# First period of the last layers, batch beside batch, and the loads and gathers ahead of it

## What is computed

```
x = LN(x + attn0(x));  x = LN(x + xattn0(x, ctx));  x = LN(x + experts(x))       # layer 0, top 2 of 8 experts
x = LN(x + attn1(x));  x = LN(x + xattn1(x, ctx));  x = LN(x + mixer(x))         # layer 1: "the last layers"

attn1: xn = layernorm(x) * g + b
  q, k = l2norm(xn Wq), l2norm(xn Wk), both rotated (rope);  v = xn Wv
  gcp  = exp(clip(cumsum(-softplus(xn Wgate + bg)), -60, 50))
  pe   = exp(p - max over tokens of p) * softplus(xn Wclock + bc),   p = xn Wp + bp
  q = q * gcp / (cumsum(pe) + 1e-8);   k = k * pe / (gcp + 1e-8)
  out = causal softmax(q k / 4) v per head (16 heads of 16);  x1 = out Wo + bo + x
  result = x1 + MLP(layernorm(x1))
```

## Time and profile before

| what | us |
|---|---|
| median of 3 runs | 1316.02 (1314.69 to 1317.96) |
| profiled execution, its own time | 1315.13 |
| its span, first to last instruction | 1313.1 |
| PE busy | 1121.8 (85%) |
| DVE busy | 738.3 (56%) |
| ACT busy | 537.9 (41%) |
| POOL busy | 454.8 (35%) |

### The profile page before, as it was taken

How to read it: one execution, slowest core, us unless ns; L and a number is a source line. 1 busy time by engine, 2 the same in 40 slices (tenths; PEclk the granted TensorE clock), 3 DMA queues, 4 the chain that set the end, 5 groups by cost and what they waited for, 6 DMA issues and landing times. The chain is left out here.

```text
span 1313.1 us, 20231 instructions
## 1 busy us (share of the span) xinstructions
PE 1121.8 (85%) x6714; PEld 786.2 (60%) x6714; DVE 738.3 (56%) x2210; ACT 537.9 (41%) x1385; POOL 454.8 (35%) x548
## 2 busy tenths in 40 slices
PE   7889988997898886899999734776997899899996
PEld 3456456545644665899999712543664575467775
DVE  1472476248435825465555427657549676846366
ACT  1371255217323711333333125464465556534541
POOL 0150034005201576666666343224132522222022
PEclk9999999999999997899999957698998999899999
DMA  5000200020001040811111170001000100000000
GB/s 190 17 1 1 55 17 1 0 55 17 1 0 55 1 158 17 301 49 50 50 49 49 34 229 8 25 1 30 3 9 1 32 2 24 1 1 25 0 1 32
DMA packets 40226, 52.37 MB, mean 40 GB/s; under 512 B 10780, under 2 KB 33372, under 8 KB 40124
## 3 DMA queue, kind: packets, MB, share of 16 engines
q1 hardware_dynamic: 31100, 36.66, 8.8%
q0 software_dynamic: 3408, 9.31, 2.5%
q10 hardware_dynamic: 5616, 5.11, 1.2%
HBM read 41.76 MB, written 9.31 MB: 39 GB/s over the span
## 5 line engine op out<-in xcount | busy, mean ns | idle before, releaser
L1281 PE MATMUL bank<-words 128*128 128x256 f32 (+3 forms) x848 | 275.4, 476 | 31.7 <-ACT words L1792 17.3
L1281 PEld LDWEIGHTS bank<-words 128*128 128x128 f32 (+1 forms) x848 | 159.7, 195 | 122.0 <-issue 66.9
L358 PE MATMUL bank<-words 128*128 128x512 f32 x384 | 173.1, 602 | 8.3 <-DMA words<-in_wq 8.3
L324 POOL TENSOR_TENSOR words<-words 128x256 f32<-128x256 f32 (+1 forms) x128 | 103.6, 831 | 190.5 <-DVE words L700 190.5
L876 PEld LDWEIGHTS bank<-words 128*128 128x128 f32 x1248 | 147.7, 194 | 4.2 <-ACT words L910 2.3
L876 PE MATMUL bank<-words 128*128 128x128 f32 x1248 | 148.2, 278 | 1.6 <-ACT words L910 1.6
L571 ACT ACTIVATE words<-words 128x128 f32<-128x128 f32 (+1 forms) x256 | 113.3, 444 | 50.2 <-DVE words L695 50.2
L358 PEld LDWEIGHTS bank<-words 128*128 128x128 f32 x384 | 72.5, 193 | 90.6 <-issue 90.0
L553 ACT ACTIVATE words<-bank 128x512 f32<-128x512 f32 x48 | 28.7, 598 | 192.5 <-PE bank L358 192.5
L925 ACT ACTIVATE words<-words 128x1024 f32 x39 | 41.2, 1057 | 146.4 <-PE bank L876 113.1
L610 DVE COPY words<-bank 128x512 f32<-128x512 f32 x48 | 33.2, 691 | 106.2 <-PE bank L358 105.9
(11 more groups left out here) (263 smaller groups left out, 2035.5 us busy)
## 6 DMA issues: line engine op xcount, KB each, us to landing
words<-in_w SPq DMA_DIRECT2D x8, 1024.0 KB
y_slots<-words ACTq DMA_DIRECT2D x39, 128.0 KB
words<-in_w SPq DMA_DIRECT2D x8, 512.0 KB
words<-in_xt SPq DMA_DIRECT2D x4, 512.0 KB, 3.8
words<-in_x SPq DMA_DIRECT2D x4, 512.0 KB, 4.2
x_rows<-words SPq DMA_DIRECT2D x16, 128.0 KB
words<-in_wm SPq DMA_DIRECT2D x2, 1024.0 KB, 6.5
out_x<-words SPq DMA_DIRECT2D x16, 128.0 KB, 1.8
```

What stands on the lines that cost most here:

```text
L324: last = pool.tensor_tensor(part, part, inv[:, j % SLOTS0, :, t:t + 1].to_broadcast([P, 2, P * (t + 1)]), ALU.mult)
L358: last = pe.matmul(bank[c % 2][:, :], w, r, start=k == 0, stop=k == KD - 1)
L1281: last = pe.matmul(out, w, r, start=i == 0, stop=i == len(pairs) - 1)
```

## The change

1. **Loads moved.** The ten loads of `rows` and `early` stand at the end of SP's queue in the experts' block, into a region at the top of SBUF that is kept free (`Memory.limit`). POOL's copy of the slots and the memsets of `minus_half` and `eps` stand at the end of its queue in that block.
2. **Boundary.** The experts' block is opened with `no_gpsimd_drain=True`.
3. **Gathers by tile.** The gathers' order is tile by tile, both choices of a tile together. In period 0 DVE takes statistics and normalises by halves (`front_half`, `front_rows_of`); for group 1 too, in two halves.
4. **Roots.** The second norm's variance is worked out on DVE (v/(v+eps)+eps, four small steps of which each has a drain ahead of it); POOL makes both roots in one `pow` (`front_rstd`). This holds for every group.
5. **Constants.** POOL writes them after the two roots of period 0; `va` waits for the four normalised tiles. ACT and DVE still wait for `const` ahead of the forms' reads and the gate; PE no longer ahead of the first turn.
6. **Period 0 by batches.** Forms, gates, factors and attention of period 0 are written out for batch 0 and batch 1, on all engines, each step on 256 columns; DVE's factors of batch 1 stand between the minima of batch 0. Rotated tiles, squares and q/k banks get places of their own (`firstra`, `firstrb`, `firstsq`, `FIRSTQK`), since batch 0's attention runs while batch 1's are alive.
7. Periods 1 to 3 keep their order; their counts are shifted (`forms_of`, `gates_of`, `squares_of`).

```diff
-        block = ctx.enter_context(nc.Block())
+        block = ctx.enter_context(nc.Block(no_gpsimd_drain=True))
...
+            for name in ("bm1", "cols", "rope", "parity"):
+                part = keep["l_" + name]
+                sp.dma_start(part[:, :] if name in ("bm1", "parity") else part[:, :, :], dram[name]).then_inc(keep["rows"], 16)
...
+            for name in ("wgate", "wclock", "wpp", "wqk", "wv1"):
+                sp.dma_start(keep["l_" + name][:, :, :], dram[name].rearrange("(k p) n -> p k n", p=P)).then_inc(keep["early"], 16)
...
-                for n in range(2 * NT):
+                for n in (r * NT + t for t in range(NT) for r in range(2)):
...
+            def front_rstd(g, b=None):
+
+                h = tiles_of(b)
+                pool.wait_ge(n3.stats, front_count(g, b))
+                pool.tensor_tensor(powers[:, 2:4, h], powers[:, 0:2, h], minus_half[:, 2:4, h], ALU.pow).then_inc(n3.rstd, 1)
+
+            front_rstd(0, 0)
+            front_rstd(0, 1)
+            constants()
+            pool.wait_ge(rows, NR * 16)
+            for b in range(GB):
+                pool.wait_ge(uready, b + 1)
+                pool.tensor_tensor(csum[:, :, batch(b)], csum[:, :, batch(b)], clog[:, :, batch(b)], ALU.add).then_inc(clogged, 1)
+                for t in range(NT)[rows_of(b)]:
+                    pool.wait_ge(turning, t + 1)
+                    pool.tensor_tensor(firstrb[:, t, :], firstrb[:, t, :], firstra[:, t, :], ALU.add).then_inc(swung, 1)
+            pool.wait_ge(vmm, NT)
+            gather(1)
...
+            for b in range(GB):
+                pe.wait_ge(turning, HALF * b + HALF)
+                first_turns(b)
+                pe.wait_ge(qkt, HALF * b + HALF)
+                for j in range(PAIRS1 // GB + 3):
+                    if j < PAIRS1 // GB:
+                        scores(0, (PAIRS1 // GB * b + j,))
+                    if j >= 3 and j % 2:
+                        weighted(0, QUADS1 // GB * b + (j - 3) // 2)
+            turn_front(1)
...
+            act.wait_ge(const, 1)
+            first_forms(0)
             front_turned(0, 1)
+            first_rows(0)
+            first_gate(0)
+            first_forms(1)
+            first_factors(0)
+            first_rows(1)
+            first_gate(1)
+            for j in range(PAIRS1):
+                if j >= 4 and j % 2 == 0:
+                    heads_copy(0, (j - 4) // 2)
+                if j == PAIRS1 // GB:
+                    first_factors(1)
+                exponential(0, j)
...
+            for t in range(HALF):
+                combine(0, t)
+                combine(0, NT + t)
+            front_half(0, 0)
+            combine(0, 2)
+            combine(0, NT + 2)
+            front_rows_of(0, 0)
+            combine(0, 3)
+            combine(0, NT + 3)
+            front_half(0, 1)
+            front_rows_of(0, 1)
...
             dve.wait_ge(const, 1)
+            first_gate(0)
+            first_max(0)
+            square_sums(0, 0)
+            first_clock(0)
+            square_sums(0, 1)
+            first_norms(0)
+            first_sums(0)
+            first_gate(1)
+            first_keys(0)
+            first_rotations(0)
+            first_max(1)
+            first_factors(0)
+            minimum(0, 0)
+            minimum(0, 1)
+            square_sums(0, 2)
+            minimum(0, 2)
+            minimum(0, 3)
+            first_clock(1)
+            minimum(0, 4)
+            square_sums(0, 3)
+            minimum(0, 5)
+            first_norms(1)
+            first_sums(1)
+            minimum(0, 6)
+            minimum(0, 7)
+            first_keys(1)
+            first_rotations(1)
+            first_factors(1)
+            for j in range(PAIRS1 // GB, PAIRS1):
+                minimum(0, j)
+                combine(1, j - PAIRS1 // GB)
+            front_statistics(1)
+            front_normalise(1)
```

More of the change, by code:

```diff
@@ new lines, in first_rows, with first_gate @@
+            def first_rows(b):
+                square(0, HALF * b)
+                value_copy(0, HALF * b)
+                value_copy(0, HALF * b + 1)
+                act.wait_ge(pmaxed, b + 1)
+                for c in range(KD):
+                    last = act.activation(pexps[:, c, batch(b)], pexps[:, c, batch(b)], ACT.Exp, bias=pmax[:, GB * c + b:GB * c + b + 1])
+                last.then_inc(pexp, 1)
+                square(0, HALF * b + 1)
+            def first_gate(b):
+                part = batch(b)
+                act.wait_ge(clr, b + 1)
+                act.activation(gabs[:, :, part], gsum[:, :, part], ACT.Exp, scale=-1.0)
+                act.drain()
+                act.activation(gabs[:, :, part], gabs[:, :, part], ACT.Ln, bias=tiny[:, :])
+                act.drain()
+                act.activation(gabs[:, :, part], gabs[:, :, part], ACT.Exp, scale=-1.0).then_inc(ginv, 1)
@@ new lines, in _, with first_gate @@
+            for t in range(HALF):
[9 more added lines that the diff above has]
+            front_rows_of(0, 1)
+            def first_gate(b):
+                dve.wait_ge(lgate, b + 1)
+                for m in range(KD):
+                    dve.tensor_tensor_scan(gsum[:, m, batch(b)], gsum[:, m, batch(b)], gabs[:, m, batch(b)], 0.0, ALU.add, ALU.add)
+                dve.drain()
+                dve.tensor_scalar(gsum[:, :, batch(b)], gsum[:, :, batch(b)], -50.0, 60.0, ALU.max, ALU.min).then_inc(clr, 1)
@@ new lines, in first_clock, with first_sums @@
+            def first_clock(b):
+                dve.drain()
+                dve.wait_ge(clogged, b + 1)
+                dve.tensor_tensor(csum[:, :, batch(b)], csum[:, :, batch(b)], qfac[:, :, batch(b)], ALU.subtract)
+            def first_sums(b):
+                dve.drain()
+                dve.wait_ge(pexp, b + 1)
+                dve.tensor_tensor(pexps[:, :, batch(b)], pexps[:, :, batch(b)], csum[:, :, batch(b)], ALU.mult)
+                dve.drain()
+                for m in range(KD):
+                    last = dve.tensor_tensor_scan(qfac[:, m, batch(b)], ones[:, :], pexps[:, m, batch(b)], 0.0, ALU.mult, ALU.add)
+                last.then_inc(sumr, 1)
@@ L2251, in _ @@
+            for p in range(1, PERIODS):
                 a, r, z = stages(p)
```

378 lines of the change are left out of this document (250 added, 128 removed).

## The result

The changed kernel takes 1304.49 us (median of 4 runs, 1303.3 to 1306.38), the one before 1316.92 in the same comparison (4 runs): ratio 0.9916, 95% interval 0.9902 to 0.9931, 12.4 us less (by the interval 9.1 to 12.9). The forecast was 1301, 15.3 less, in a range of 1294 to 1310. The profiled execution of the changed kernel has a span of 1304.6 and a time of 1306.38, 1.9 over its median.

A forecast was written before the change was run, and what follows sets the result against it. No engine was taken as the bound, but an order in which batches 0 and 1 pass each step together. 1315.13 - 3.3 (boundary) - 12.0 (period 0's stages) = 1299.8, set to 1301 us for the median; range 1294 to 1310.

The forecast's parts named there:

- The boundary: Between last y store and first gather: taking out the drain saves 3.3 us, bounds 0 and -3.7.
- The entry: Last block's first instruction to ACT's first read of a form: 20.5 us instead of 27.7, saving 7.2.
- `const` is late next: End of the entry: POOL's constants come last, and ACT waits 6 us for them.
- Forms to scores: ACT's first read of a form to batch 0's first scores: 31.8 us instead of 47.5, saving 15.7.
- The clamp beside POOL's sum: Forms to scores, on DVE: clamp priced at 1.2 us from the trace; by the page alone, 0.2.
- Scores to period 1: First scores to period 1's first product: 45.9 us instead of 35.0, costing 10.9, with batch 1's factors between batch 0's minima.
- Periods 1 to 3: After period 0: order kept, gains stay; DVE's extra small steps in periods 1 and 2 cost 0, bounds -2 and +2.
- The first two: Period 0's TensorE clock: 1.2 GHz all through, 1314.7 us, chance 0.12; or staying at 2.4 GHz, 1295 us, chance 0.12.
- what the prediction held against cutting them: Products cut in halves: idle gaps between short bursts bring TensorE's clock back down, by the Trainium skill's rule.
- The second: Rival: TensorE stays at 2.4 GHz in period 0; batch 1's quads save 3.2 us, the rest 2.5; 1295 us, chance 0.12.
- The third: Rival at the boundary: the wait isn't removed but moves; 1304 us, chance 0.08.
- The fourth: Rival in period 0: batches don't overlap, 8.5 us more, and bursts stay at 1.2 GHz; 1323 us, chance 0.05.

The follow-up runs named there:

- e10: Kernel before with only the experts' block ended without its GpSimd drain: 1313.40 us, ratio 0.9994.
- e1: Changed kernel with only the experts' block closed by its GpSimd drain again: 1307.64 us, ratio 0.9946.
- e9: Kernel before with one added POOL drain in the experts' block, ahead of its wait for the last y stores: 1312.33 us, ratio 0.9982.
- e2: Changed kernel with the ten loads issued at the start of the last layers' block again: 1310.76 us, ratio 0.9967.
- e3: Changed kernel with the gathers' order back to all first rows, then all second rows: 1311.97 us, ratio 0.9974.
- e5: Changed kernel with POOL's constants between the two halves' powers, without their wait for the normalised tiles: 1304.93 us, ratio 0.9918.
- e7: Changed kernel with one more TensorE product into an unused bank behind each of period 0's 16 score steps: 1329.17 us, ratio 1.0112.
- e8: Changed kernel with all eight minima of batch 0 ahead of batch 1's work in DVE's order in period 0: 1310.94 us, ratio 0.9968.
- e11: e5 with group 1's eight gathers on POOL moved ahead of batch 1's first rotation sum: 1305.24 us, ratio 0.9928.

## Why the prediction held, and where it did not

**The boundary.** -3.3 was the right size: the first gather stands 2.8 us behind DVE's last sum for 6.4. The reason given was wrong, so this term came out right by luck. "The drain that the change takes out stands there" is true (3.26 us in the sequencer's records), but the step from there to the gain fails: taken out alone it is worth nothing at the boundary (e10), put back alone it costs 0.1 (e1), since the next drain behind the gathers takes the wait over. The step that I priced at nothing, the three POOL instructions moved ahead of the wait, brings the gain through the drain that ends it (e9). The trace of before alone could not show that, as its second drain, behind the copy, takes 0.25.

**The entry.** From T0 to ACT's first read 27.7 to 21.3, forecast 20.5. Gathers are 1.25 apart, the first half's power starts at +10.5 and the constants end it at +21.2; 0.6 of the miss is the first gather, at T0 + 0.7 and not + 0.1. The loads' wait was a real cost (e2: 2.4), the order of the gathers as well (e3: 1.9). That `const` is late next was right; dropping its wait alone gives 1.8 at the read and nothing at the end (e5).

**Forms to scores.** 31.87 us, forecast 31.8. The gate came at T0 + 29.6 (28.7), batch 1's at + 43.6 (42.6), the scores at + 53.1 (52.3). The clamp beside POOL's sum was rightly priced from the trace (1.31 us for 1.2); in the kernel before, too, it stands beside the add (814.35 and 814.34) and not behind it. The prediction read the Trainium skill, GPSIMD Engine Reference, 8. Key points, too narrowly there: beside those of two SBUF inputs the section names DVE instructions in a 2-port perf mode as contending with POOL. Whether the clamp runs in that mode the trace does not say; in the kernel before DVE's one-input step of 128x1024 from SBUF to SBUF takes 0.66 us (at 811.74) and its two-input one of the same shape 1.23, which fits it. So the page gave no ground for leaving the clamp at 0.2.

**Scores to period 1.** 46.5 us, forecast 45.9: 22.35 between the batches' first scores (22.1), and 14.1 from there to the last minimum's end (14.1). The granted clock went as forecast: 0.5 up to T0 + 28, 1.0 to the scores, then 0.63 on the mean. Together T0 to period 1 takes 99.6 for 110.2, -10.6 where the sum had -12.0.

**Periods 1 to 3** are the term that failed: 0 with bounds -2 and +2, measured +3.5. "Four small steps more and POOL five less", priced at 0, costs 1.0 in period 1, as the steps stand ahead of a minimum in DVE's queue and POOL's are not on the path. 2.1 more come from the clock, which steps down at other points of the later periods. I had no such term; the rows of before show only where the clock fell there. "What is won by then should stay won" was not true to a microsecond.

By the traces the sum is then -3.3 - 10.6 + 3.5 = -10.4. The medians have -12.4, with an interval of -9.1 to -12.9 that holds both. The two profiled executions lie 1.8 below and 1.9 above their medians; 2.0 of that stand ahead of the last layers (the dip at 303).

**Rivals.** The first two (clock all low, all high) did not come: the steps fell where the forecast had them. The forms cut in halves ran at 1.00 from 782 to 806, so what the prediction held against cutting them did not come. The second's price cannot be had by feeding TensorE (e7). The third is refuted by the first gather's place in the changed kernel, but it describes e10 exactly. The fourth, batches one behind the other, is e8: 4.6 us between the batches, not 8.5, and the time was 1311, not 1323.

## What to carry to other kernels

A drain of POOL behind its own gathers is paid once, by the first that comes: put it ahead of a wait that is there anyway. Between two serial chains, interleaving in DVE's queue was worth 4.6 us at its own place, more than the loads (2.4), the gathers' order (1.9) or the drain (3.3) at theirs, though in the whole time e8 (6.8) is no worse than e2 (6.7) or e3 (7.6). Each microsecond won at the entry has to pass a stage whose clock and late results vary by 3 us, so judge a piece at the stage where it works and not by the end alone. Before moving a POOL clear or sum, look at what DVE does beside it.

## What was not expected of the hardware

- The first drain of POOL behind 39 gathers ends 3.3 us after POOL's last instruction, at the block's end, behind the copy and ahead of the wait alike. Its records are 3.26, 3.47, 4.59 and 4.79 long (before, e10, e9, changed) only because they start while the copy or the last sum still runs. Behind eight gathers it is 0.7, with none since the last drain 0.04.
- TensorE's results came 1.7 to 4.5 us late in seven of ten variants while POOL issued gathers, and followed them when they were moved (e11, one trace).
- A DVE step beside POOL can last until POOL is done: the two clamps end 0.05 to 0.06 us behind POOL's sum, one started with it and one 0.62 later; POOL's clear of 2048 elements stretched two one-input steps from 0.73 to 2.80 us, and eight sums in a row two steps of two inputs from 1.32 to 6.95 (e7).
- With TensorE busy 3.80 of 4 us or more, 32-row scores mixed with 128-row products, the granted clock stayed at 0.50 for 20 us (e7, 808 to 828), while the products of the stage before ran at 1.00 with TensorE busy 2.60 to 3.71 of 4 us (e7, 780 to 800).
